# Two row operations of the next batch moved from GpSimd to ScalarE, and GpSimd's steps for it to later slots

## What is computed

```python
x = L0_attn_x                                   # 8 x 512 x 256
xn = _layernorm(x, axis=-1)
x = x + _L0_attn_ref(xn, Wq, Wk, Wv) + _L0_ffn_ref(xn, gate_w, w1, w2)
xn = _layernorm(x, axis=-1)
x = x + _L1_attn_ref(xn, ...) + _L1_ffn_ref(xn, weight, bias)

def _layernorm(x, axis=-1, eps=1e-05):
    m = jnp.mean(x, axis=axis, keepdims=True)
    v = jnp.var(x, axis=axis, keepdims=True)
    return (x - m) / jnp.sqrt(v + eps)

# Mamba block, per batch, 512 channels, 16 states
u = silu(conv(x) + conv_b);  delta = softplus(...)
h = exp(delta * A) * h + delta * B * u          # one step of the scan
y = sum over states of h * C;  out = (y + u * D) * silu(z) @ out_proj
```

## Time and profile before

| | |
|---|---|
| median of 3 runs | 2385.25 us (2382.43 to 2387.0) |
| the profiled execution | 2384.27 us, its span 2382.5 us |
| mean granted clock of TensorE | 0.903 of full speed |
| TensorE busy | 1790.6 us (75%) |
| VectorE (DVE) busy | 1579.1 us (66%) |
| GpSimd (POOL) busy | 1053.2 us (44%), nearly all of it in the mix block |
| ScalarE (ACT) busy | 963.4 us (40%) |
| waits of the drives (line 1146) on the sums | 169.3 us |
| waits of the decays (line 1255) on the reads | 312.0 us |
| waits of the scans (line 1370) on decays and drives | 49.8 and 45.3 us |

### The profile page before, as it was taken

One profiled execution on the slowest core, in us unless ns is written; L12 is line 12 of the kernel. 1 busy time (PEld: TensorE's weight loads), 2 busy tenths in 40 slices (PEclk: granted clock), 3 DMA queues, 4 the chain that ended last, 5 costly groups with the idle time before them and its releaser, 6 DMA issues.

```text
span 2382.5 us, 20828 instructions
## 1 busy us (share of the span) xinstructions
PE 1790.6 (75%) x6312; PEld 842.6 (35%) x6312; DVE 1579.1 (66%) x1836; ACT 963.4 (40%) x1480; POOL 1053.2 (44%) x740
## 2 busy tenths in 40 slices
PE   7569696978869695969446877777877778877776
PEld 6333433434433433334112242332423324242333
DVE  6336362636445362636149989798988989889896
ACT  3106152433425161423343634536354463644632
POOL 2600000000000000000368896978879698796962
PEclk9879897999979797989669998999899999998999
DMA  4513232313123232321230130402204040030300
GB/s 174 197 60 103 74 103 78 112 55 136 42 68 108 75 102 72 106 67 44 79 151 0 62 106 3 150 18 97 72 2 150 19 150 18 34 118 10 141 9 9
DMA packets 81804, 189.11 MB, mean 79 GB/s; under 512 B 8161, under 2 KB 60514, under 8 KB 69970
## 3 DMA queue, kind: packets, MB, share of 16 engines
q1 hardware_dynamic: 78674, 180.06, 22.0%
q0 software_dynamic: 3072, 8.37, 1.1%
HBM read 151.72 MB, written 36.70 MB: 79 GB/s over the span
## 4 chain that ended last, share of the span: by engine, by line
DVE 12%; POOLq 12%; POOL 10%; PE 10%; issue 5%; DVEq 1%; ACT 1%
DVE ps L1370 6%; PE ps L1479 5%; POOLq L1118 3%; POOL work L1146 3%; POOLq L1194 3%; DVE work L1376 3%; POOL xn L1122 2%; POOLq L1137 2%; POOLq L1135 2%; POOL e_rows L1120 2%; DVE u L1361 2%; PE ps L1487 1%; PE ps L1459 1%; DVE absmax L1343 1%; POOL e_rows L1081 1%
## 5 line engine op out<-in xcount | busy, mean ns | idle before, releaser
L1479 PE MATMUL ps<-work,ident_sb 128*128 128x512 f32 x1024 | 541.7, 655 | 205.6 <-DVE work L1376 205.3
L1146 POOL TENSOR_TENSOR work<-bc,du 128x1024 f32<-128x1024 f32 x256 | 602.1, 2365 | 171.2 <-PE ps L1479 169.3
L1370 DVE TENSOR_TENSOR_SCAN ps<-ps,work 128x1024 f32<-128x1024 f32 x256 | 585.5, 2287 | 95.3 <-ACT ps L1255 49.8
L697 DVE TENSOR_REDUCE m<-ps 128x1 f32<-128x512 f32 x512 | 327.2, 686 | 300.3 <-PE ps L803 298.7
L1255 ACT ACTIVATE ps<-delta,a_neg 128x512 f32<-128x512 f32 x512 | 331.6, 682 | 312.7 <-DVE work L1376 312.0
L1479 PEld LDWEIGHTS ps<-work,ident_sb 128*128 128x128 f32 x1024 | 197.5, 205 | 493.4 <-DVE work L1376 319.8
L620 ACT ACTIVATE prob<-ps 128x1024 f32<-128x1024 f32 x256 | 256.7, 1021 | 234.4 <-PE ps L827 232.3
L561 POOL TENSOR_TENSOR m_parts<-m,nil 128x16 bf16<-128x16 f32 x32 | 7.1, 222 | 736.7 <-DVE m L697 736.7
L803 PE MATMUL ps<-k_st,q_st 96*128 96x512 bf16 x512 | 185.1, 408 | 193.9 <-DMA k_st<-qk_parts 171.7
L1376 DVE TENSOR_TENSOR work<-ps,bc 128x1024 f32<-128x1024 f32 x256 | 308.6, 1206 | 0.0
L1459 PE MATMUL ps<-xn_t,in_w 128*128 128x512 f32 x256 | 141.8, 687 | 54.8 <-DVE u L1361 35.9
(11 more groups left out here) (168 smaller groups left out, 2086.4 us busy)
## 6 DMA issues: line engine op xcount, KB each, us to landing
bc<-bc_rows SPq DMA_DIRECT2D x64, 1024.0 KB, 4.7
w<-in_w SPq DMA_DIRECT2D x32, 1024.0 KB
qk_parts<-parts SPq DMA_DIRECT2D x96, 128.0 KB
q_st<-qk_parts SPq DMA_DIRECT2D x16, 384.0 KB
k_st<-qk_parts SPq DMA_DIRECT2D x16, 384.0 KB
dispatch<-zeros SPq DMA_DIRECT2D x4, 1280.0 KB, 10.5
x_in<-in_x SPq DMA_DIRECT2D x8, 512.0 KB, 3.6
rows<-dispatch SPq DMA_DIRECT2D x32, 128.0 KB
```

The lines of the kernel that those rows point to most:

```text
L697: nc.vector.tensor_reduce(m[:, g % 2, qt, 2 * pair + i:2 * pair + i + 1], ps[:, S0 + i, :], AX.X, ALU.max).then_inc(s_reduced, 1)
L1146: nc.gpsimd.tensor_tensor(work[:, n % WS, :, :], bc[:, j, 0, :, :], du[:, b % 2, c, :].unsqueeze(1).broadcast_to([P, PAIR, SEQ]), ALU.mult ...
L1370: nc.vector.tensor_tensor_scan(s, s, work[:, n % WS, :, :].rearrange("p i t -> p (i t)"), 0.0, ALU.mult, ALU.add).then_inc(state_ready, 1)
L1479: x = nc.tensor.matmul(ps[:, YB, :], sb["ident"][:, :], work[:, n % WS, i, :], start=False, stop=(n % PAIRS == PAIRS - 1 and i == PAIR - 1))
```

## The change

`weigh_experts` and `normalise` leave GpSimd's list and enter ScalarE's. The first becomes four copies with the gate as scale, in slot 2 behind decay 2. The second becomes four identities with `rstd` as scale and `shift` = -mean * `rstd` as bias, in slot 9 behind decay 9. `shift` is new; `root` computes it on GpSimd with two more operations on four columns. Two semaphores are new: `e_weighed` (ScalarE to GpSimd, ahead of the add) and `rstd_ready` (GpSimd to ScalarE, ahead of the normalising). GpSimd's add goes from slot 4 to slot 8 and loses its drain, its root from slot 10 to slot 12. VectorE's, TensorE's and SyncE's lists are the same. For batch 0, both operations stand on ScalarE behind the diagonals `d_diag` (line 1262).

```diff
-ACT_AT = {"out": (6, 10), "w": 3, "first_quant": (4, 5), "turned": (11, 12), "x": (13, 14, 15, 16), "silu_u": 18, "bc": 19,
+ACT_AT = {"weigh": 2, "normalise": 9, "out": (6, 10), "w": 3, "first_quant": (4, 5), "turned": (11, 12), "x": (13, 14, 15, 16), "silu_u": 18, "bc": 19,
...
-POOL_AT = {"gather": 0, "weigh": 3, "add": 4, "root": 10, "normalise": 11, "down": 16, "grid": 22, "up": 27, "input": 28}
+POOL_AT = {"gather": 0, "add": 8, "root": 12, "down": 16, "grid": 22, "up": 27, "input": 28}
...
-                def weigh_experts(f):
-                    pool.wait_ge(e_gathered, (f + 1) * TT * 16)
-                    for t in range(TT):
-                        nc.gpsimd.tensor_scalar(e_rows[:, t, :], e_rows[:, t, :], gate_cur[:, t:t + 1], None, ALU.mult)
-
                 def add_experts(f):
-                    pool.drain()
+                    pool.wait_ge(e_weighed, f + 1)
                     pool.wait_ge(x1_loaded[f % XS], f // XS * 16 + 16)
...
                 def root(f):
                     pool.wait_ge(moments_ready, f + 1)
+                    if f:
+                        pool.wait_ge(xn_ready, f)
                     nc.gpsimd.tensor_tensor(rstd[:, :], moments[:, :, 1], eps[:, :], ALU.add)
                     pool.drain()
                     nc.gpsimd.tensor_tensor(rstd[:, :], rstd[:, :], neg_half[:, :], ALU.pow)
+                    nc.gpsimd.tensor_scalar(shift[:, :], moments[:, :, 0], -1.0, None, ALU.mult)
                     pool.drain()
-
-                def normalise(f):
-
-                    if f:
-                        pool.wait_ge(quant_turned, f * KD)
-                    for t in range(TT):
-                        r = nc.gpsimd.tensor_scalar(xn[:, t, :], x2[:, f % XS, t, :], moments[:, t, 0:1], rstd[:, t:t + 1],
-                                                    ALU.subtract, ALU.mult)
-                    r.then_inc(xn_ready, 1)
+                    nc.gpsimd.tensor_tensor(shift[:, :], shift[:, :], rstd[:, :], ALU.mult).then_inc(rstd_ready, 1)
...
             @block.scalar
             def _(act):
+                def weigh_experts(f):
+                    act.wait_ge(e_gathered, (f + 1) * TT * 16)
+                    for t in range(TT):
+                        r = nc.scalar.activation(e_rows[:, t, :], e_rows[:, t, :], ACT.Copy, scale=gate_cur[:, t:t + 1])
+                    r.then_inc(e_weighed, 1)
+
+                def normalise(f):
+
+                    act.wait_ge(rstd_ready, f + 1)
+                    if f:
+                        act.wait_ge(quant_turned, f * KD)
+                    for t in range(TT):
+                        r = nc.scalar.activation(xn[:, t, :], x2[:, f % XS, t, :], ACT.Identity, scale=rstd[:, t:t + 1], bias=shift[:, t:t + 1])
+                    r.then_inc(xn_ready, 1)
+
...
+                weigh_experts(0)
+                normalise(0)
                 for k in range(KD):
                     copy_turned(0, k, k)
...
+                        if q == ACT_AT["weigh"]:
+                            weigh_experts(f)
+                        if q == ACT_AT["normalise"]:
+                            normalise(f)
```

More of the change, by code:

```diff
@@ L945, in mix_block @@
         rstd = buf("rstd3", [P, TT])
+        shift = buf("shift", [P, TT])
         xn = buf("xn3", [P, TT, DM])
@@ L977, in mix_block @@
         e_gathered = sem("e_gathered")
+        e_weighed = sem("e_weighed")
+        rstd_ready = sem("rstd_ready")
         x1_loaded = [sem(f"x1_loaded_{i}") for i in range(XS)]
@@ L1153, in _ @@
                 gather(0, range(TT))
-                weigh_experts(0)
                 add_experts(0)
                 root(0)
-                normalise(0)
                 scale_down(0)
@@ L1176, in _ @@
                             gather(f, range(2, TT))
-                        if q == POOL_AT["weigh"]:
-                            weigh_experts(f)
                         if q == POOL_AT["add"]:
@@ L1182, in _ @@
                             root(f)
-                        if q == POOL_AT["normalise"]:
-                            normalise(f)
                         if q == POOL_AT["down"]:
```

## The result

The changed kernel takes 2408.4 us (median of 10 runs) against 2383.2 us for the kernel before (10 runs): a ratio of 1.0113, 95% interval 1.0088 to 1.0139. It is 25 to 27 us slower; 31 were forecast, 2417 with a range of 2402 to 2436.

A forecast was written before the change was run, and what follows sets the result against it. Bound: GpSimd's chain from grid to add, plus VectorE's from statistics to binade. 7 x (5.1 + 4.0 - 3.4 - 0.7) = +35 us, less 3.8 once, gives +31: 2417 us, range 2402 to 2436.

The forecast's parts named there:

- What bounds the kernel: Mix-stage period of 145.0 us: GpSimd's chain from grid to add, plus VectorE's chain from statistics to binade.
- Part 1: GpSimd's add, slot 4 to 8: ends behind four more drives, VectorE's statistics wait; +5.1 us a period.
- The cover: VectorE's 7 us stand in slot 4 hides the weighing's 0 to 2 us delay of decay 3 and scan 3.
- Parts 2 and 3: Scan 10 late: 2.4 us from ScalarE's normalising behind drive 12, 1.8 from TensorE's low clock at sum 3; mean 4.0.
- Part 4: VectorE's scaling of `absmax`, slot 11: wait shrinks, gain 1.3 or 3.4 us a period, 3.4 taken; convolution wait another 0.7.
- Part 5: First batch: add starts 1.35 us earlier, normalising and signal save 2.4; -3.8 us once.
- The sum: Whole kernel: seven periods' terms give +35 us, less 3.8 once: +31 us.
- (1): Rival: scan 10 late, `absmax` scaling still waits for a drive; 2437 us, or 2425 with clock kept; chance 0.24.
- (2): Rival: GpSimd's relief counts in full, early drives repay the stand; 8.0 us off each period, 2325 us; chance 0.07.
- (3): Rival: no effect; stand in slot 4 and wait in slot 9 are paid for by 8.5 us; chance 0.04.
- (4): Rival: activation table loads before both ScalarE groups and again before the next decay; over 2440 us; chance 0.03.
- some 1.0 added: GpSimd's new work per period, subtracted from 3.65, 0.50 and 4.85 us to give its relief of about 8.0 us.

The follow-up runs named there:

- `e3_late_add`: The kernel before with only GpSimd's add moved from slot 4 to slot 8: ratio 1.0229 to the kernel before, 56 us slower.
- `e5b_busy6`: The changed kernel with 6 idle zero-matrix products on TensorE in slot 4, filling the stand: period 2.4 us shorter than in the changed kernel.
- `e2_norm`: The kernel before with only the normalising moved to ScalarE (slot 9) and root in slot 12; weighing and add as before: ratio 0.9936 to the kernel before.
- `e1_add4`: The changed kernel with GpSimd's add put back to slot 4: 2342.0 us, ratio 0.982 to the kernel before.
- `e9_root9`: The changed kernel with GpSimd's root in slot 9 instead of 12: ratio 1.0094 to the kernel before.
- `e6_odd`: The kernel before with the scaling of `absmax` over 33 columns instead of 32: ratio 0.9988 to the kernel before.
- `e6b_unequal`: The kernel before with the scaling of `absmax` over 33 columns, read as 3 x 11 and written as 11 x 3: the scaling takes 4.1 us again.

## Why the prediction was right, point by point

- **What bounds the kernel** held. GpSimd's half and VectorE's half follow each other, and what is put into either shows in the period: `e3_late_add` adds 9.2 us to the first half, and the period grows by 8.75.
- **Part 1**, the later add: +5.1 forecast, +5.0 measured (26.8 against 21.8 us from slot 0 to the statistics). The cover was as forecast: the weighing starts at 1976.28, 3.3 us after GpSimd has issued the last gather and gone on with drive 2 (1972.98), and delays scan 3 by 0.35 us, in front of a stand of 6.66 us.
- **Parts 2 and 3**, the normalising behind drive 12 and the low clock: +4.0 forecast, +4.4 measured (27.7 against 23.3). The run with the filled stand puts 1.8 of it to the clock, where the forecast had 1.6 as the mean. What is left is 2.6, against 2.4. In the period shown scan 10 is 26.2 us behind the add's end, 5.3 later than before, where 4.2 was the term and 4.6 its upper bound. Three sizes were short. The products behind sum 3 are at the low clock as well, so that sum 6 is done 2.5 us later behind the add, not 1.8. From the end of drive 12 to the signal it takes 2.3 instead of 1.95 (a gap of 0.48 before the power; it is 0.48 or more in all nine profiled runs in which the weighing has left GpSimd, and 0.14 in the five in which it has not, `e2_norm` among them; why is open). And the normalising takes 2.08 instead of 1.95. One path was not seen either, though TensorE has no gap from sum 3 to sum 6, so that it can't have made scan 10 later. ScalarE's `copy_out` in slot 6 waits 5.32 us for the output projection, which is late behind the slow sum; decay 7 is queued behind it, and scan 7 waits 1.37 us for that.
- **Part 4**, the scaling: -3.4 forecast, -3.4 measured (3.56 to 0.18 in all seven). Which of two values it would be hung on two starts 0.3 us apart. The value taken was right because sum 9 is slow after its gap of 3.33 us, so that drive 15 starts at 2025.44, behind the scaling at 2024.49 (0.4 to 1.5 us behind it in the seven periods). The prediction tied this to "the low clock of part 3", and that tie is not there: in `e1_add4` and `e5b_busy6` sum 3 has no low clock and the scaling takes 0.18 all the same, since sum 9 follows the same gap of 3.33 us. It is the wait of scan 10 that makes the gap, and `e9_root9`, without that wait, has the 2.2 us again. The further gain behind it is 1.0 us where I took 0.7.
- **Part 5**, the first batch: -3.8 forecast, -4.6 measured. `xn` is ready 3.2 us earlier (less than worked out, by the sizes above), and drive 0 gains 1.4 more on the way, where GpSimd waits less for ScalarE's logarithm. That 1.4 may be chance: in the four kernels with the old steps for batch 0 (`before`, `e3_late_add`, `e6_odd`, `e6b_unequal`) the same length is 78.0 to 79.7.
- **The sum**: +31 forecast and +30.9 in the two profiles from the attention's end on. The medians say +25, with an interval from +21 to +33: the forecast lies in it.
- **Rivals.** (1), the scaling still waiting, did not happen in the changed kernel, but does with root in slot 9: the two parts are coupled as it said. (2) and (3), the stand paid back, fall with `e3_late_add`. (The "some 1.0 added" to GpSimd in the sum and in (2) does not agree with part 2's own 0.4; measured is 0.7.) (4), table loads, fell too: the normalising's row is followed by its decay without one.

## What to carry to other kernels

A step that is moved to a later slot in a fixed order is late by all the work put in front of it, if its engine is the one that the next half waits for; count what it stands behind, not what it costs. Work can leave a busy engine and still be a loss when it takes the signal out of the order: here a weighing moved alone was worth 1.5%, and the same weighing, with the normalising moved too and the add four slots later, cost 1.1%. A tiny instruction that takes 20 times its own length beside another engine's work is worth a look at its form, if its engine is the one that the period waits for.

## What the runs showed of the hardware that I had not expected

- VectorE's scaling of 128x32 (0.18 us alone) can wait past the end of the product under way on GpSimd: in the kernel before it took 2.43 to 4.59 us in six of seven periods, until the next product too had ended, which was the last before a gap. In the seventh it took 1.77 and came in at the end of the product under way, with another right behind it. So it may wait for more than one product, but need not wait for a gap. An unequal outer size of source and destination (11 x 3 read, 33 written) makes it 0.19 us beside a running product.
- A fp32 product of 128x512 with its 128x128 weights is issued as two instructions, 0.44 us apart at the full clock (1.00 granted): 12 products made 24 in 10.46 us.
- 5.3 us of products with zeros in a gap of 7 us kept the granted clock at 1.00, so that the next sum took 1.99 us instead of 3.78, although TensorE stood idle for 1.72 us between them. It was so in six of seven periods (idle for 1.1 to 1.8 us); in the first, where 4.31 us of idle time lay between the same filling and the sum, the granted clock was 0.50 in the sum and it took 3.78.
